# Attention products in blocks of three pairs, a second engine for the softmax sums of two passes, and key copies one a step

## The reference

```python
att = softmax(einsum('bthd,bshd->bhts', q, k) * HD ** -0.5)   # spatial; temporal (causal); cross
o = einsum('bhts,bshd->bthd', att, v)
x = x + fused                                                   # cross attention's output projection
x = x + gelu(ln(x) @ mlp_w1.T + b1) @ mlp_w2.T + b2
```

## Time and profile before

| | us |
|---|---|
| median of 3 runs (1834.28 to 1839.62) | 1836.44 |
| the profiled execution's own time | 1838.64 |
| its span | 1836.6 |
| its mean granted TensorE clock | 0.965 of full speed |
| PE busy | 1652.5 (90%) |
| DVE busy | 1066.6 (58%) |
| POOL busy | 875.5 (48%) |
| ACT busy | 711.8 (39%) |

### The profile page before, as it was taken

How to read it: one execution, slowest core, us unless ns; L and a number is a source line. 1 busy time by engine, 2 the same in 40 slices (tenths; PEclk the granted TensorE clock), 3 DMA queues, 4 the chain that set the end, 5 groups by cost and what they waited for, 6 DMA issues and landing times. The chain is left out here.

```text
span 1836.6 us, 32041 instructions
## 1 busy us (share of the span) xinstructions
PE 1652.5 (90%) x10735; PEld 1378.3 (75%) x10735; DVE 1066.6 (58%) x2221; ACT 711.8 (39%) x1346; POOL 875.5 (48%) x815
## 2 busy tenths in 40 slices
PE   2899988876899999999999997899999996899998
PEld 1788757755777888778878876788788874797896
DVE  7778768885556445654564562665555555683332
ACT  1223211114666445556555552464546553120010
POOL 3213001102587657684644466156566689383440
PEclk9999999988999999999999998899999998999999
DMA  3101000011031100030000000000000002121111
GB/s 116 35 7 47 12 1 29 18 49 50 12 125 41 35 19 7 1 130 12 18 13 7 7 1 24 17 19 7 7 13 13 1 1 85 40 74 35 46 35 56
DMA packets 24788, 58.06 MB, mean 32 GB/s; under 512 B 2537, under 2 KB 4805, under 8 KB 24013
## 3 DMA queue, kind: packets, MB, share of 16 engines
q1 hardware_dynamic: 24650, 56.18, 9.5%
HBM read 44.87 MB, written 11.30 MB: 31 GB/s over the span
## 5 line engine op out<-in xcount | busy, mean ns | idle before, releaser
L1801 DVE TENSOR_REDUCE max_part<-ps 125x2 f32<-125x500 f32 x520 | 328.1, 674 | 224.9 <-PE ps L2318 199.9
L1380 ACT ACTIVATE p_raw<-ps 125x500 f32<-125x500 f32 x520 | 296.9, 586 | 280.7 <-PE ps L2361 271.8
L1088 POOL TENSOR_TENSOR p_sum<-p_sum,p_raw 125x500 f32<-125x500 f32 x200 | 232.5, 1163 | 222.9 <-ACT p_raw L1380 215.7
L2376 PE MATMUL ps<-p_raw,v_rows 125*64 125x250 f32 x2080 | 248.5, 380 | 0.0
L1090 POOL TENSOR_TENSOR p_sum<-p_sum,p_raw 125x500 f32<-125x500 f32 x200 | 232.5, 1163 | 15.7
L2376 PEld LDWEIGHTS ps<-p_raw,v_rows 125*64 125x64 f32 x2080 | 143.4, 137 | 73.5 <-issue 4.5
L1641 DVE TENSOR_SCALAR onehot<-iota_h,win_key,key_t 125x320 f16 x453 | 176.9, 390 | 0.5 <-issue 0.4
L1817 DVE RECIPROCAL feat<-ps 128x250 f32<-128x250 f32 x60 | 103.0, 1717 | 113.8 <-PE ps L2386 113.6
L2260 PE MATMUL ps<-xa_hi,w_hi 128*128 128x418 f32 (+1 forms) x448 | 150.1, 335 | 14.5 <-POOL w_lo L954 9.1
L2357 PE MATMUL ps<-q_both_a,k_both_a 128*125 128x250 f32 x520 | 154.3, 317 | 9.4 <-ACT p_raw L1380 7.6
L2318 PE MATMUL ps<-k_both_a,q_both_a 128*125 128x250 f32 x520 | 143.8, 292 | 20.6 <-issue 9.1
(11 more groups left out here) (395 smaller groups left out, 3723.0 us busy)
## 6 DMA issues: line engine op xcount, KB each, us to landing
w_raw<-in_w_mlp SPq DMA_DIRECT2D x32, 256.0 KB, 2.7
w_raw<-in_w_gps SPq DMA_DIRECT2D x16, 256.0 KB, 2.6
w_raw<-in_w_tp SPq DMA_DIRECT2D x16, 256.0 KB, 2.6
w_raw<-in_w_sp SPq DMA_DIRECT2D x12, 256.0 KB, 2.7
w_raw<-in_w_cr SPq DMA_DIRECT2D x12, 256.0 KB, 2.6
d_xt<-xb_hi SPq DMA_DIRECT2D x1, 2508.0 KB, 9.4
d_xt<-xb_lo SPq DMA_DIRECT2D x1, 2508.0 KB, 15.0
xa_hi<-d_xt SPq DMA_DIRECT2D x1, 2508.0 KB, 9.3
```

The source lines that it names most:

```text
L1088: pool.tensor_tensor(total, total, halves[0], ALU.add).then_inc(s_add, 1)
L1380: act.activation(p_raw[:, g % PR, :], ps[0:TOK, g % 2, 0:4 * TOK], ACT.Exp, scale=SCALE).then_inc(s_exp, 1)
L1801: dve.tensor_reduce(part[:, y, :, j], ps[0:TOK, bank, 0:4 * TOK].rearrange("p (h k) -> p h k", h=2), AX.X, ALU.max)\
L2376: ins = pe.matmul(ps[r, bank, 0:2 * TOK], v_rows[:, n % 2, kt, h, :], p_raw[:, (g - 1 + h) % PR, cols], start=(b == 0 and x == 0), stop=last)
```

## The change

1. `BLOCK_PAIRS` goes from 2 to 3. 132 blocks (4 of one pair, 128 of two) become 91 (4 of one, 5 of two, 82 of three). The instructions stay the same in number; products and denominators move later between the scores.
2. In passes 7 and 11 (`SHARED`) POOL adds only head 0 (125x250), and DVE adds head 1 in `add_second_head`, at the start of each step with h = 1, with a semaphore of its own. Exponent and denominator wait for both.
3. ACT makes one of the two key copies a step: head 0 one step after K, head 1 two steps after.

```diff
-BLOCK_PAIRS = 2
+BLOCK_PAIRS = 3
+SHARED = (7, 11)
@@ POOL, add_pair
-                total = p_sum[:, u % 2, :, :]
-                halves = [p_raw[:, (g - 1) % PR:(g - 1) % PR + 2, 2 * TOK * x:2 * TOK * (x + 1)] for x in range(2)]
-                pool.wait_ge(s_exp, g + 1)
+                heads = 1 if n in SHARED else 2
+                total = p_sum[:, u % 2, 0:heads, :]
+                halves = [p_raw[:, (g - 1) % PR:(g - 1) % PR + heads, 2 * TOK * x:2 * TOK * (x + 1)] for x in range(2)]
+                pool.wait_ge(s_exp, g - 1 + heads)
@@ ACT, the step loop
+                    if g > first + 1:
+                        for task in SIDE[g - 2]:
+                            third_out(task)        # key_copy(n, p, 1); second_out does key_copy(n, p, 0)
@@ ACT, exponent
                     act.wait_ge(s_add, ADD_NO[n, i, b])
+                    if n in SHARED:
+                        act.wait_ge(s_add_b, SHARED_NO[n, i, b])
@@ DVE
+            def add_second_head(g):
+                n, i, b, _ = STEP[g]
+                u, done = 5 * n + i, SHARED_NO[n, i, b]
+                total = p_sum[:, u % 2, 1, :]
+                halves = [p_raw[:, g % PR, 2 * TOK * x:2 * TOK * (x + 1)] for x in range(2)]
+                dve.wait_ge(s_exp, g + 1)
+                if b == 0:
+                    dve.wait_ge(s_den, u - 1)
+                    dve.tensor_tensor(total, halves[0], halves[1], ALU.add).then_inc(s_add_b, 1)
+                else:
+                    dve.wait_ge(s_add_b, done - 2)
+                    dve.tensor_tensor(total, total, halves[0], ALU.add).then_inc(s_add_b, 1)
+                    dve.wait_ge(s_add_b, done - 1)
+                    dve.tensor_tensor(total, total, halves[1], ALU.add).then_inc(s_add_b, 1)
                 for g in range(first, end):
+                    if STEP[g][0] in SHARED and STEP[g][3] == 1:
+                        add_second_head(g)
@@ PE, denominator
+                if n in SHARED:
+                    pe.wait_ge(s_add_b, SHARED_NO[n, i, blocks_in(n, i) - 1])
```

More of the change, by code:

```diff
@@ L182 @@
 ADDED = [(n, i, b) for n in range(PASSES) for i in range(5) for b in range(blocks_in(n, i))]
+SHARED = (7, 11)
+SHARED_NO = {(n, i, b): 2 * x + 2 - (5 * y + i + 1) for y, n in enumerate(SHARED) for x, (m, i, b) in
+             [(x, at) for x, at in enumerate(at for at in ADDED if at[0] in SHARED) if at[0] == n]}
 ADD_NO = {(n, i, b): 2 * x + 2 - (5 * n + i + 1) for x, (n, i, b) in enumerate(ADDED)}
@@ L717, in build @@
         s_add = sem("s_add")
+        s_add_b = sem("s_add_b")
         s_den = sem("s_den")
@@ L1298, in key_hi, with key_copy @@
                 ins.then_inc(s_k_hi, 1)
-            def key_copy(n, p):
+            def key_copy(n, p, h):
                 cols = slice(NP * p, NP * p + NP)
                 act.wait_ge(s_k_hi, 3 * n + p + 1)
-                for h, r in enumerate(HALF):
-                    ins = act.activation(k_both[h][HALF[1 - h], n % 2, cols], f32(k_both[h][r, n % 2, cols]), ACT.Copy)
-                ins.then_inc(s_k_both, 1)
+                act.activation(k_both[h][HALF[1 - h], n % 2, cols], f32(k_both[h][HALF[h], n % 2, cols]), ACT.Copy).then_inc(s_k_both, 1)
             def query_bias(n):
@@ L1401, in second_out, with third_out @@
                 if what == "K":
-                    key_copy(*at)
+                    key_copy(*at, 0)
                 if what == "Q":
                     query_copy(*at)
+            def third_out(task):
+                what, *at = task
+                if what == "K":
+                    key_copy(*at, 1)
             act.wait_ge(s_ld_ev, 32)
@@ L1426, in _ @@
                 query_hi(n, 0)
-                key_copy(n, 0)
-                key_copy(n, 1)
-                key_copy(n, 2)
+                for p in range(3):
+                    for h in range(2):
+                        key_copy(n, p, h)
                 value_feat(n, 0)
@@ L2314, in maximum @@
                 pe.wait_ge(s_q_lo, 5 * n + i + 1)
-                pe.wait_ge(s_k_both, 3 * n + 3)
+                pe.wait_ge(s_k_both, 6 * n + 6)
                 for h in range(2):
```

## The result

The changed kernel takes 1840.02 us, the median of 20 runs (1838.55 to 1846.11), beside 1837.9 us for the kernel before: a ratio of 1.0015, 95% interval [1.0008, 1.0022]. I had forecast 1826, against a kernel before of 1836.4 (three runs). It is a little slower, so the gain went somewhere. The profiled execution after took 1846.11 us, the longest of the 20 and 6 us over their median (span 1844.0), against 1838.64 before. So lengths within it overstate the loss: the profiled executions lie 7.5 us apart, the medians 2.1. Where that matters, other runs with the same lists are put beside it.

What follows compares the result with a forecast made beforehand. PE, busy 90% of the span, was taken as the bound. Terms of -10.7 + 6 - 2 - 6 + 1 = -11.7, rounded to -11, gave a forecast of 1826 us, range 1812 to 1840.

Steps and rivals of the forecast that it cites:

- Fewer blocks, saved: On PE, 41 blocks fewer save 0.26 us of transition each: -10.7 us, between -9 and -12.
- Fewer blocks, lost: PE loses cover: +4 at exponent waits, +3 in the openings (passes 0 and 8), -1 at Q chains; together +6.
- the longer stretch without products: Rival, at steps between blocks in the ten unshared passes: ACT and DVE exposed, waits grow by half, +12, 1848 us; chance 0.14.
- the fifth more: Expected in the changed profile: PE's waits for the exponent more in number by a fifth.
- Key copies: One key copy a step on ACT delays fewer exponents that PE waits for: -2 us, between -4 and +1.
- Pass 7: PE's 9.61 us wait for POOL shrinks to about 3, low clock partly goes, DVE costs 2.5: -6 us, -11 to 0.
- Pass 11: POOL wait and low clock go (-6.7), but DVE's additions and tok_z spend the gain: +1 us, between -8 and +7.
- The sum: Whole kernel: the terms make -11.7 us, rounded to -11, so 1826 us from the median.
- wrong if: Signs: ten unshared passes not shorter, DVE holding PE over 8 us in pass 11, or projection closely following the last product.
- The third: Sign of error after pass 11: the projection's start stands closer than 10 us to the last product.

Runs made afterwards that it cites:

- g4: The changed kernel with one-pair blocks, 260 in all: 1835.95 us, ratio 0.9987 to the kernel before.
- g3: The changed kernel, but two-pair blocks where a block begins in pass 0 or 8, three-pair blocks elsewhere: 1826.91 us, ratio 0.9938 to the kernel before.
- e4: The changed kernel with BLOCK_PAIRS = 2 again, so sharing and split copies without longer blocks: 1826.96 us, ratio 0.9938 to the kernel before.
- h2: The changed kernel, but three-pair blocks only where a block begins in pass 0 or 8, two-pair elsewhere: 1839.12 us, ratio 1.0000 to the kernel before.
- e2: The kernel before with only the sharing of additions between POOL and DVE in passes 7 and 11: 1831.29 us, ratio 0.9958.
- e3: The kernel before with only one key copy a step: 1832.04 us, ratio 0.9962.
- h1: The changed kernel with thrown-away matmuls ahead of the second unit's first score in passes 0 and 8: 1836.50 us, ratio 0.9993 to the kernel before.
- g1: The changed kernel with two-pair blocks and most of DVE's tok_z instructions moved later: 1820.78 us, ratio 0.9907 to the kernel before.
- i3: The changed kernel with two-pair blocks (three-pair in passes 1, 11), later tok_z, ACT-list moves, thrown-away matmuls in five waits: 1813.24 us, ratio 0.9870 to before.

## Why the prediction was wrong, step by step

- **Fewer blocks, saved (-10.7).** About right in size. A pair more costs 0.85 us, a transition some 0.27 (g4).
- **Fewer blocks, lost (+6, +2 to +14).** This step failed. With 14.2 us net and 10.7 saved, it was about +25. Two terms in it: in the ten passes other than the openings the loss is 33 x 0.26 = 8.6 us, since g3 equals e4, where I had +3 (+4 and -1). In the openings I had +3; h2 against e4 and after against g3 give 12 and 13 net by the medians, with 8 or 9 x 0.26 saved, so about +15. I had written that "those scores wait for ACT anyway, so the 1.84 us of product come on top". That counted the block, but not that the longer block ahead starves ACT first (2.14 us), nor that the lower clock follows the longer wait (4 to 7 us in the two openings).
- **The rival** of the longer stretch without products was the right mechanism (ACT exposed, slower). It was placed wrong for the greater part: about 15 of the 25 us stand in the two openings, where ACT has a burst of side work, and only 8.6 at all other steps together, where it had put the whole loss. The waits for the exponent went from 62 to 75, the fifth more that I had named, and in time from 33.8 to 39.1 us, a sixth more, not the half of the rival.
- **Key copies (-2, -4 to +1).** Under-sized: -7.0 alone, -3.7 on top of sharing (e4 against e2). In pass 9 one wait went from 1.79 us (before) to 1.10 (e3), and with it a stretch of low clock (0.83 and 1.00 over ten us; the wait, then the stretch before and in e3):

```profile
1321.18 0.44 PE L2357 MATMUL ps<-q_both_b,k_both_b 128*125 128x250 f32 x1 [1.79 <-ACT p_raw L1380]
```

```profile
1318.00:1328.00 10.00, 8.21 (x53) 6.36 (x52) 3.58 (x6) 4.67 (x9) 4.62 (x4) 0.83 0.00 0
```

```profile
1312.00:1322.00 10.00, 8.90 (x72) 7.04 (x69) 5.28 (x8) 4.66 (x11) 4.84 (x6) 1.00 0.00 0
```

- **Pass 7 (-6, -11 to 0).** Its direction was right. Alone (e2) it is -10.1: the wait fell to 2.19 us and no low clock followed. In the changed kernel it is -3.1, and 2 of the missing 7 us are chance: g3 and h1 have the same lists there and the same wait (3.50), but 117.9 and 118.2 us, -5.4 and -5.1, because the lower clock took less of the pass (10.5 and 9.6 us, against 16.4 after). The other 5 are the three-pair blocks (g3 against e4). The prices were near: POOL's half addition 0.69 to 0.82 (0.64 and 0.2 for DVE's), DVE's 0.67 to 0.88 (0.75).
- **Pass 11 (+1, -8 to +7).** Right within its range. e2 gives -1.8 in the pass and +5.1 behind it, so +3.4. I had the place: the last additions behind `tok_z`. I had `tok_z` at 1 us each; beside POOL's additions four took 5.69, and an addition 1.4 to 1.5.
- **The sum.** With measured sizes: -7.7 and -7.0 alone, -11.4 together, +14.2 for the blocks, which is +2.8. That -11.7 was rounded to -11 and not -12 changes nothing here. Without the failed step, the rest errs the other way: sharing and copies gave 11.4 where I had 7. Of the signs that I had named as "wrong if", one came plainly: the ten passes longer. DVE held the last denominator for 10.11 us, but over 8 us was also what I expected there, so this sign could tell nothing. The third didn't come: the projection started 19.6 us after the last products began.

## What to carry over

Batching work on the bound engine saves a fixed price per batch, but work placed between dependent steps is also cover. Ask of each batch what the other engines do while it runs and what covers their bursts when it is gone; here over half of the loss sat in two of twelve passes, where side work bunches. Where an instruction list is strictly in order, put what the last result waits for ahead of work that is merely ready.

## What the runs showed of the hardware

- The clock is a second price of long waits, and not a steady one. In the profiled executions of before, after, e4 and g1, every idle time of PE of 3.49 us and more that is shown above was followed by the lower level. For a shorter one the length alone doesn't tell: 2.60 us ahead of 489.78 left the clock up, 1.79 us ahead of 1321.18 (before, pass 9) did not. And the same wait costs differently from one execution to the next. Behind the wait of 3.5 us in pass 7 the lower level lasted until 6.3 us after its end in the kernel after (1133.08) and until 3.1 us after it in g3. In h1 the denominator still ran at the upper level (0.64 us, not 1.10), and the lower stood from 0.9 to 4.3 us after the wait. The first row is g3's, the second h1's:

```profile
1124.57 1.10 PE L2422 MATMUL ps<-p_sum,ones_f 125*64 125x250 f32 x4 [3.50 <-POOL p_sum L1097]
```

```profile
1128.56 0.64 PE L2429 MATMUL ps<-p_sum,ones_f 125*64 125x250 f32 x4 [3.50 <-POOL p_sum L1096]
```

- Matmuls whose result is thrown away kept the clock up and gave some 4 to 5 us (h1, i3), although they do nothing.
- The clock also fell with PE never idle, among 32 matmuls of two columns that ran from 667.1 to 671.6 us (`bo_parts`). Before, from 670 us:

```profile
670.00:672.00 2.00, 2.00 (x11) 2.00 (x11) 0.20 (x2) 0.00 (x0) 0.00 (x0) 0.50 0.00 0
```

- DVE and POOL reading SBUF together: DVE pays more. DVE's 125x250 addition takes 0.42 us alone. At the end of pass 11 in e4, where POOL adds to `tok_z` without a break, one instruction each 1.40 us, it takes 1.36 to 1.47. POOL's half additions (lines 1093 and 1095) take 0.71 and 0.62 where DVE is idle, 0.82 and 0.69 on average in the shared stretch of pass 7. The Trainium skill (SBUF — State Buffer, section "Who interferes with whom") has the two exclude each other. The times agree: at the end of pass 11 each of DVE's four additions ends 0.27 us behind the end of one of POOL's instructions, while POOL's keep coming every 1.40 us.
